# Gated cross-attention block on one core: attention by half pairs in batches of four units, one layer norm pass for the latents, and the first 2 MB over two DMA queues

## The chip, the cores and the metric

The kernel runs on one core of one Trainium2 chip. The metric is device time in microseconds (us): the median of the runs. The engines are TensorE (PE in the profile, its weight loads PEld), VectorE (DVE), ScalarE (ACT), GpSimd (POOL) and SyncE (SP), which here only issues DMAs.

## The reference, cut to what matters

Shapes: x is (2, 1024, 512), the context (2, 2048, 512), 16 heads of 64.

```python
x = x + tanh(g_xattn) * xattn(_layernorm(x), ctx)          # (x - m) / sqrt(var + 1e-5)
x = x + tanh(g_ffn) * ffn_int8(_layernorm(x))              # quantised 512x512 product

# inside xattn
lat = layer_norm(latents, g, b)                            # a second norm of the normed x, then gain and bias
ctx = layer_norm(context, g, b)
q = lat @ Wq                                               # 512 -> 1024
k, v = split(ctx @ Wkv)                                    # 512 -> 2048; k gets rotary cos/sin
attn = clip(q k^T / 8, -11, 11)
out = softmax(attn) v
return out @ Wo + bo
```

So x is normalised twice in a row before q. With v the variance of x and e = 1e-5, the two passes together multiply (x - m) by 1/sqrt(v(1 + e) + e^2).

## The kernel before

Everything is float32. Products that need the precision are split: a tensor is held as a rounded part (`_hi`, type float32r) and a rest (`_lo`), and three float32r products are summed (`split_product`). The probabilities, values and row sums are plain float32, and the profile shows each such matmul as two.

There are four stages, each with a hand-written program for every engine, joined by semaphores.

**Query stage.** x comes in four chunks of 512 rows into `raw`. For each chunk DVE measures mean and variance (`measure`, bn_stats and bn_aggr), ACT takes the root (`sqrt`), DVE normalises in place (`normalise`), and all that a second time, since the reference does it twice. PE transposes the chunk into `turn_ps` (`turn`), ACT applies gain and bias (`affine`), DVE splits the result into `tok_hi` and `tok_lo` (`tok_split`), and PE makes eight q tiles of 128 columns from it. The first chunk is handled in two parts (one tile of 128 rows, then three). Wq arrives in two stages of 1 MB, each with half of the 512 rows and all 1024 columns; ACT makes `wq_hi` and POOL `wq_lo`, and the first q product waits for both stages. All loads are issued by SP. ACT first computes `gate_tanh`.

**Context stage.** Eight chunks of context give k and v, which go to scratch in DRAM. The change touches it only in names and in one place of ACT's program.

**Attention stage.** Two batches by eight pairs of heads give 16 head pairs (`ALLPAIRS`). A head pair has 16 steps of 128 keys, each against all 1024 queries. In step s, PE makes the scores of both heads (a = 0, 1) for the two query halves in two PSUM slots `score_ps[:, half]` (12 matmuls, two heads side by side on 64 rows of the array each), ACT takes the exponential of each half (128x1024) into `prob`, DVE clips the step's 128x2048 in place (`prob` L1022), PE multiplies with v (`value_ps` L874, two heads side by side on 64 columns each), and DVE adds the tile to `prob_sum` (L1013, L1016). `prob` has 4 slots, so DVE, ACT and PE may stand up to four steps apart. PE's order is scores(s), values(s-1).

After a head pair, PE sums `prob_sum` over the partitions (`sums`, L887), and the row sums take a way through DRAM: ACT copies them, SP stores them, loads them spread over 128 partitions, DVE takes reciprocals, SP stores these and loads them broadcast to 64 rows a head, DVE multiplies (`normalise`, L204), SP stores the output (`PairEnds`). SP issues the ten loads of pair n+2 (4 MB) when pair n is done, and then this chain.

In pairs 0 and 1 DVE also quantises the FFN weight (`quantise_rhs`), and POOL makes `wo_lo`.

**Output stage.** 16 tiles of 128 rows: projection by Wo, residual, norm, int8 product. The last pair's chain runs beside its first tiles.

## Time and profile before

| | us |
|---|---|
| median of 3 runs | 1541.34 |
| lowest, highest | 1540.91, 1545.64 |
| the profiled execution's own time | 1544.19 |
| its span | 1542.4 |
| PE busy | 1490.7 (97%) |
| DVE busy | 1287.8 (83%) |
| ACT busy | 714.5 (46%) |

PE's busy time counts matmuls that are pipelined, with ends that are modelled; it doesn't say that PE is at its peak. What a stretch costs is read from the starts of its instructions. The stages by time: query stage to about 130 us, context stage to 490, attention 492.5 to 1422, output stage to the end.

### The profile page before, as it was taken

What the parts mean: (1) busy time and instruction counts of PE and PEld (TensorE: products, weight loads), DVE (VectorE), ACT (ScalarE), POOL (GpSimd) and SP (SyncE); (2) the same over time, 40 slices, a digit from 0 to 9 for tenths busy, and PEclk for the clock granted to TensorE, in tenths of its full rate; (3) what the DMA queues carried; (4) which work ended last, traced back from release to release, by engine and by line L of the source; (5) the groups of instructions that cost most, each with busy time, mean ns of one, the idle gap of its engine ahead of it and who ended that gap; (6) DMA issues with size and microseconds to landing.
All of it is one profiled execution on the core that took longest, in us unless ns stands there. A gap on an engine that the chain in (4) does not pass through costs nothing. (4 is left out here: it accounts for less than half of the span.)

```text
span 1542.4 us, 22114 instructions
## 1 busy us (share of the span) xinstructions
PE 1490.7 (97%) x7896; PEld 869.5 (56%) x7896; DVE 1287.8 (83%) x1256; ACT 714.5 (46%) x794; POOL 127.8 (8%) x72
## 2 busy tenths in 40 slices
PE   3999999999999899999999999999999999999997
PEld 3788888888886334444444444444444444444774
DVE  6866666676654999899899899899899899998887
ACT  3433222222223555555555555555555555555342
POOL 2220000000000210000000000000000000000765
PEclk9999999999999999999999999999999999999998
DMA  5665655546567540541440440441441442311652
GB/s 185 232 240 190 190 164 181 161 153 200 163 181 256 142 123 29 124 115 38 123 123 28 123 123 27 123 123 38 113 123 46 105 123 55 97 42 35 185 163 82
DMA packets 121998, 195.30 MB, mean 127 GB/s; under 512 B 18368, under 2 KB 67520, under 8 KB 115808
## 3 DMA queue, kind: packets, MB, share of 16 engines
q1 hardware_dynamic: 119360, 190.49, 42.5%
q10 hardware_dynamic: 2592, 4.20, 0.7%
q8 instruction: 28, 0.46, 0.1%
q14 instruction: 18, 0.15, 0.0%
HBM read 114.70 MB, written 79.95 MB: 126 GB/s over the span
## 5 line engine op out<-in xcount | busy, mean ns | idle before, releaser
L932 ACT ACTIVATE prob<-score_ps 128x1024 f32<-128x1024 f32 x512 | 496.3, 1022 | 377.7 <-PE score_ps L861 377.5
L1016 DVE TENSOR_TENSOR prob_sum<-prob_sum,prob 128x2048 f32<-128x2048 f32 x224 | 516.0, 2304 | 0.5
L874 PE MATMUL value_ps<-prob,v_st 128*64 128x512 f32 x2048 | 496.6, 606 | 10.6 <-DVE prob L1022 10.3
L861 PE MATMUL score_ps<-q_st,k_st 64*128 64x512 f32 x3072 | 426.4, 409 | 2.5 <-PEq L102 2.1
L861 PEld LDWEIGHTS score_ps<-q_st,k_st 64*128 64x128 f32 x3072 | 269.2, 185 | 256.4 <-ACT prob L932 187.8
L1022 DVE TENSOR_SCALAR prob<-prob 128x2048 f32<-128x2048 f32 x256 | 314.0, 1226 | 68.1 <-ACT prob L932 64.2
L874 PEld LDWEIGHTS value_ps<-prob,v_st 128*64 128x64 f32 x2048 | 124.2, 136 | 250.1 <-issue 201.7
L645 DVE TENSOR_TENSOR k_cos<-k_raw,rope 128x1024 f32<-128x1024 f32 x32 | 39.2, 1225 | 99.9 <-ACT k_raw L546 99.9
L551 ACT ACTIVATE v_out<-proj_ps 128x1024 f32<-128x1024 f32 x31 | 31.9, 1030 | 136.7 <-PE proj_ps L228 136.7
L546 ACT ACTIVATE k_raw<-proj_ps 128x1024 f32<-128x1024 f32 x31 | 31.9, 1029 | 105.2 <-PE proj_ps L228 104.0
L1331 POOL MEMSET unround<- 128x1 f32 x1 | 0.1, 98 | 872.6 <-POOLq L115 872.6
L228 PE MATMUL proj_ps<-tok_hi,wkv_hi 128*128 128x512 f32 x248 | 67.0, 392 | 0.0
L228 PE MATMUL proj_ps<-wkv_lo,tok_hi 128*128 128x512 f32 x248 | 66.4, 389 | 0.0
L228 PE MATMUL proj_ps<-tok_hi,wkv_lo 128*128 128x512 f32 x248 | 66.3, 389 | 0.0
L228 PE MATMUL proj_ps<-tok_lo,wkv_hi 128*128 128x512 f32 x248 | 66.3, 389 | 0.0
L228 PE MATMUL proj_ps<-wkv_hi,tok_hi 128*128 128x512 f32 x248 | 66.3, 389 | 0.0
L228 PE MATMUL proj_ps<-wkv_hi,tok_lo 128*128 128x512 f32 x248 | 66.3, 389 | 0.0
L228 PEld LDWEIGHTS proj_ps<-tok_hi,wkv_lo 128*128 128x128 f32 x248 | 46.5, 188 | 9.7
L228 PEld LDWEIGHTS proj_ps<-wkv_hi,tok_lo 128*128 128x128 f32 x248 | 46.5, 188 | 9.7
L228 PEld LDWEIGHTS proj_ps<-wkv_lo,tok_hi 128*128 128x128 f32 x248 | 46.5, 188 | 9.7
L228 PEld LDWEIGHTS proj_ps<-wkv_hi,tok_hi 128*128 128x128 f32 x248 | 46.5, 188 | 9.7
L228 PEld LDWEIGHTS proj_ps<-tok_lo,wkv_hi 128*128 128x128 f32 x248 | 46.5, 188 | 9.7
(119 smaller groups left out, 1306.2 us busy)
## 6 DMA issues: line engine op xcount, KB each, us to landing
k_st<-k_scr SPq DMA_DIRECT2D x128, 256.0 KB, 6.2
k_scr<-k_hi SPq DMA_DIRECT2D x64, 256.0 KB, 2.7
v_scr<-v_out SPq DMA_DIRECT2D x32, 512.0 KB, 3.5
k_scr<-k_lo SPq DMA_DIRECT2D x64, 256.0 KB, 4.0
q_st<-q_scr SPq DMA_DIRECT2D x16, 1024.0 KB, 10.5
v_st<-v_scr SPq DMA_DIRECT2D x16, 1024.0 KB, 13.3
q_scr<-q_hi SPq DMA_DIRECT2D x32, 256.0 KB, 3.3
q_scr<-q_lo SPq DMA_DIRECT2D x32, 256.0 KB, 3.4
```

The costliest lines, as they stand in the source:

```text
L228: last = pe.matmul(acc, s, m, start=(n == 0), stop=(n == len(terms) - 1))
L546: act.activation(k_raw[:, j % 2, :, :], banks(what, j, order), ACT.Copy).then_inc(k_copied, 1)
L551: act.activation(v_out[:, j, :], banks(what, j, order), ACT.Copy).then_inc(v_copied, 1)
L645: last = dve.tensor_tensor(made[:, :, :], k_raw[:, s, :, :], rope[:, slot, f:f + 1, :].broadcast_to((P, 2, CH)), ALU.mult)
L861: last = pe.matmul(score_ps[:, half, a, :], k_st[slot][rows, k_part, s * P:(s + 1) * P], q_st[slot][rows, q_part, cols], start=(t == 0), s ...
L874: last = pe.matmul(value_ps[rows, cols], v_st[slot][:, s, rows], prob[:, s % PSLOT, a, cols], start=(s == 0), stop=(s == STEPS - 1))
L932: act.activation(prob[:, s % PSLOT, :, cols], score_ps[:, half, :, :], ACT.Exp, scale=SCALE).then_inc(exped, 1)
L1016: dve.tensor_tensor(total, total, prob[:, s % PSLOT, :, :], ALU.add).then_inc(added, 1)
L1022: dve.tensor_scalar(tile, tile, CLIP_LOW, CLIP_HIGH, ALU.max, ALU.min).then_inc(clipped, 1)
L1331: pool.memset(unround[:, :], -ROUND).then_inc(unround_set, 1)
```

## The change

Three things are changed at once.

**1. Attention.** The unit of work is now one step of 128 keys against 512 queries (one half), both heads. A head pair runs all 16 steps of query half 0, then all of half 1: 32 units, in 8 batches of 4. PE makes the scores of a batch (3 PSUM slots instead of 2, a wait on an exponential for each unit), then the values of the batch before. DVE clips a batch at once (128x4096) and adds it in two 128x2048 additions (one for the first batch of a half). `prob` has two slots of a batch. `value_ps` and `sum_ps` are half as wide. The additions keep two unit positions apart (j), so `sums` now runs four matmuls of 32 output columns for a half, at rows 0, 32, 64 and 96, and DVE joins the two parts before the reciprocal. The chain through DRAM runs twice a pair, once for a half, and SP issues the loads of pair n+2 between the two. `quantise_rhs` all falls into pair 0, three pieces a batch.

**2. Query stage.** One pass replaces the two norms: the root is taken of v(1 + e) + e^2. The first chunk goes tile by tile. wq_hi and wq_lo are now made by column halves (all 512 rows, 512 columns), so the first four q tiles wait only for the first half. DVE makes `wq_lo` instead of POOL. PE runs 56 transposes of the identity at the start (`keep_busy`), before the first tile is there, and 10 after the last transposed tile. The tanh of the gates moves to the end of the context stage.

**3. First loads.** The four tiles of the first chunk and the two halves of the first wq stage are issued in turns by SP and ACT.

```diff
-        for tiles, arrived in ((FRONT[0], front_in), (BACK[0], raw_in[0])):
-            sp.dma_start(raw[:, 0, tiles, :], ...
+        for t in range(0, CT, 2):
+            sp.dma_start(raw[:, 0, t, :], x[t * P:(t + 1) * P, :]).then_inc(front_in[t], 16)
+        load_stage(0)
         sp.dma_start(gains[:, :, :], affines).then_inc(gains_in, 16)
-        load_stage(0)
         load_stage(1)
...
     @block.scalar
+        for t in range(1, CT, 2):
+            act.dma_start(raw[:, 0, t, :], x[t * P:(t + 1) * P, :]).then_inc(front_in[t], 16)
+        load_wq_piece()
...
     @block.vector
-        for p in range(2):
-            measure(0, 0, p, p == 1, FRONT)
-            measure(0, 0, p, p == 1, BACK)
-            normalise(0, p, FRONT)
-            normalise(0, p, BACK)
+        for i, part in enumerate(SINGLE):
+            measure(0, 0, part)
+            if i:
+                normalise(0, 0, SINGLE[i - 1])
+        normalise(0, 0, SINGLE[-1])
+        wq_rest(0)
         tok_split(0, 0)
-        measure(1, 1, 2, False)
+        wq_rest(1)
+        measure(1, 1)
...
     @block.tensor
         pe.wait_ge(ident_set, 2)
-        turn(0, 0)
-        pe.wait_ge(w_hi_made, 2)
+        keep_busy(WARM_EARLY)
+        turn_singles()
+        keep_busy(WARM_LATE)
...
 attention, PE
-        def scores(n, slot, s):
+        def scores(n, slot, b):
-            for half in range(2):
-                g = 2 * (STEPS * n + s) + half
-                if not (first(n) and s == 0):
-                    pe.wait_ge(exped, g - 1)
+            for u in range(b * BATCH_UNITS, (b + 1) * BATCH_UNITS):
+                half, s = divmod(u, STEPS)
+                cols = slice(half * CH, (half + 1) * CH)
+                if u >= BANKS:
+                    pe.wait_ge(exped, UNITS * n + u - BANKS + 1)
...
-        def values(n, slot, s):
+        def values(n, slot, b):
+            pe.wait_ge(clipped, BATCHES * n + b + 1)
+            for i in range(BATCH_UNITS):
+                s = (b * BATCH_UNITS + i) % STEPS
                 for a in range(2):
+                    last = pe.matmul(value_ps[rows, :], v_st[slot][:, s, rows], prob[:, b % 2, i, a * CH:(a + 1) * CH],
...
+        def sums(n, half):
+            for j in range(2):
                 for a in range(2):
+                    row = (2 * j + a) * SUM_ROWS
+                    last = pe.matmul(sum_ps[row:row + SUM_ROWS, :], ones[:, 0:SUM_ROWS], prob_sum[:, half, j, a, :],
...
 attention, DVE
+        def clip(n, b):
+            tile = prob[:, b % 2, :, :]
+            dve.wait_ge(exped, UNITS * n + (b + 1) * BATCH_UNITS)
+            dve.tensor_scalar(tile, tile, CLIP_LOW, CLIP_HIGH, ALU.max, ALU.min).then_inc(clipped, 1)
...
 attention, SP
+        def after(n, where, before, loading=None):
+            ends.store_sums(sp, n, 0)
+            ends.load_sums(sp, n, 0)
+            if before is not None:
+                ends.store_output(sp, n - 1, 1, *before)
+            ends.store_reciprocals(sp, n, 0)
+            ends.load_reciprocals(sp, n, 0)
+            if loading is not None:
+                load(n + 2, *loading)
+            ends.store_sums(sp, n, 1)
+            ends.load_sums(sp, n, 1)
+            ends.store_output(sp, n, 0, *where)
+            ends.store_reciprocals(sp, n, 1)
+            ends.load_reciprocals(sp, n, 1)
```

PE's program at the start of the query stage, before. Each row is a line, an operation, output and inputs, the output's shape and how many in a row:

```order
L681 MATMUL turn_ps<-ident,raw 128x128 x4
L687 MATMUL turn_ps<-ident,raw 128x128 x12
L228 MATMUL proj_ps<-tok_hi,wq_hi 128x512 x4
L228 MATMUL proj_ps<-tok_hi,wq_lo 128x512 x4
L228 MATMUL proj_ps<-tok_lo,wq_hi 128x512 x4
```

And now:

```order
L684 MATMUL proj_ps<-ident 128x128 x56
L690 MATMUL turn_ps<-ident,raw 128x128 x16
L684 MATMUL proj_ps<-ident 128x128 x10
L230 MATMUL proj_ps<-tok_hi,wq_hi 128x512 x4
L230 MATMUL proj_ps<-tok_hi,wq_lo 128x512 x4
L230 MATMUL proj_ps<-tok_lo,wq_hi 128x512 x4
```

Transposes of the identity stand ahead of and behind the 16 of the first chunk; the q products are the same.

PE's program in pair 1 of the attention, around the sums of pair 0, before:

```order
L861 MATMUL score_ps<-q_st,k_st 128x512 x12
L874 MATMUL value_ps<-prob,v_st 64x512 x4
L887 MATMUL sum_ps<-prob_sum,ones 64x512 x4
L861 MATMUL score_ps<-q_st,k_st 128x512 x12
L874 MATMUL value_ps<-prob,v_st 64x512 x4
```

And now:

```order
L888 MATMUL score_ps<-q_st,k_st 128x512 x24
L900 MATMUL value_ps<-prob,v_st 64x512 x8
L888 MATMUL score_ps<-q_st,k_st 128x512 x24
L900 MATMUL value_ps<-prob,v_st 64x512 x8
L914 MATMUL sum_ps<-prob_sum,ones 32x512 x4
L888 MATMUL score_ps<-q_st,k_st 128x512 x24
L900 MATMUL value_ps<-prob,v_st 64x512 x8
```

Score and value matmuls now change places half as often, with 24 and 8 in a row for 12 and 4; the sums stand twice a pair, on 32 columns for 64.

DVE's program in a late pair of the attention, before:

```order
L1016 TENSOR_TENSOR prob_sum<-prob_sum,prob 128x2048
L1022 TENSOR_SCALAR prob<-prob 128x2048
L1016 TENSOR_TENSOR prob_sum<-prob_sum,prob 128x2048
L204 TENSOR_TENSOR o_out<-o_raw,recip 128x512
L1022 TENSOR_SCALAR prob<-prob 128x2048
```

And now, for the first half of a pair:

```order
L1050 TENSOR_SCALAR prob<-prob 128x4096
L1062 TENSOR_TENSOR prob_sum<-prob 128x2048
L1050 TENSOR_SCALAR prob<-prob 128x4096
L1066 TENSOR_TENSOR prob_sum<-prob_sum,prob 128x2048 x2
L206 TENSOR_TENSOR o_out<-o_raw,recip 128x512
L1050 TENSOR_SCALAR prob<-prob 128x4096
L1066 TENSOR_TENSOR prob_sum<-prob_sum,prob 128x2048 x2
L1050 TENSOR_SCALAR prob<-prob 128x4096
L1066 TENSOR_TENSOR prob_sum<-prob_sum,prob 128x2048 x2
L192 TENSOR_TENSOR sum_both<-sum_sq 128x8
L197 RECIPROCAL rec_sq<-sum_both 128x8
```

A half has 4 clips of double width and 7 additions; a whole pair had 16 clips and 15 additions.

## Rows read from the trace of the kernel before

**Rows 1.** Timeline of PE: start, us, engine, line, instructions; sums of pairs 1 and 5.

```profile
627.06 1.89 PE L887 MATMUL sum_ps<-prob_sum,ones 128*64 128x512 f32 x8
...
855.34 1.89 PE L887 MATMUL sum_ps<-prob_sum,ones 128*64 128x512 f32 x8
```

**Rows 2.** Timeline of one attention step; some rows from narrower windows.

```profile
803.54 1.65 PE L861 MATMUL score_ps<-q_st,k_st 64*128 64x512 f32 x12
804.35 0.62 PE L861 MATMUL score_ps<-q_st,k_st 64*128 64x512 f32 x4
804.58 0.19 PEld L861 LDWEIGHTS score_ps<-q_st,k_st 64*128 64x128 f32 x2
804.63 1.94 ACT L932 ACTIVATE prob<-score_ps 128x1024 f32<-128x1024 f32 x2 [0.67 <-PE score_ps L861]
805.13 1.94 PE L874 MATMUL value_ps<-prob,v_st 128*64 128x512 f32 x8
805.61 0.14 PEld L874 LDWEIGHTS value_ps<-prob,v_st 128*64 128x64 f32 x2 [0.29 <-issue]
806.04 0.14 PEld L874 LDWEIGHTS value_ps<-prob,v_st 128*64 128x64 f32 x2 [0.28 <-issue]
807.00 1.67 PE L861 MATMUL score_ps<-q_st,k_st 64*128 64x512 f32 x12
```

**Rows 3.** Timeline of DVE in the last pair, where an addition follows its own clip.

```profile
1377.24 1.22 DVE L1022 TENSOR_SCALAR prob<-prob 128x2048 f32<-128x2048 f32 x1
1378.49 2.29 DVE L1016 TENSOR_TENSOR prob_sum<-prob_sum,prob 128x2048 f32<-128x2048 f32 x1
...
1401.59 0.69 DVE L204 TENSOR_TENSOR o_out<-o_raw,recip 128x512 f32<-128x512 f32 x1
```

**Rows 4.** Timeline of pair 0 and the first sums.

```profile
492.52 1.66 PE L861 MATMUL score_ps<-q_st,k_st 64*128 64x512 f32 x12 [2.11 <-PEq L102]
506.21 4.47 DVE L1016 TENSOR_TENSOR prob_sum<-prob_sum,prob 128x2048 f32<-128x2048 f32 x1
567.55 1.89 PE L887 MATMUL sum_ps<-prob_sum,ones 128*64 128x512 f32 x8
```

**Rows 5.** DVE by line and form, 500 to 640 us: count, busy us, mean ns.

```profile
L985 DVE TENSOR_REDUCE rhs_amax<-rhs_raw 128x1 f32<-128x512 f32 x4 | 2.7, 670 | 0.0
L1001 DVE TENSOR_SCALAR rhs_raw<-rhs_raw 128x512 f32<-128x512 f32 x4 | 1.7, 415 | 0.0
```

**Rows 6.** Timeline of SP in one pair: sums stored, then loaded.

```profile
804.12 2.16 SPq L157 DMA_DIRECT2D sum_scr<-sum_row  x1
810.10 0.40 SPq L162 DMA_DIRECT2D sum_sq<-sum_scr  x1
```

**Rows 7.** Timeline of the query stage's start.

```profile
10.57 1.91 ACT L485 ACTIVATE wq_hi<-w_stage 128x2048 fp32r<-128x2048 f32 x1
10.91 1.46 DVE L592 TENSOR_SCALAR raw<-raw,meanvar,rstd 128x512 f32<-128x512 f32 x3
17.48 5.73 DVE L592 TENSOR_SCALAR raw<-raw,meanvar,rstd 128x512 f32<-128x512 f32 x3
27.93 2.04 PE L228 MATMUL proj_ps<-tok_hi,wq_hi 128*128 128x512 f32 x4 [1.84 <-DVE tok_hi L601]
34.54 1.09 PE L228 MATMUL proj_ps<-tok_hi,wq_lo 128*128 128x512 f32 x4
39.12 1.07 PE L228 MATMUL proj_ps<-tok_hi,wq_hi 128*128 128x512 f32 x4
```

**Rows 8.** Timeline of PE: the transposes of chunks 1 and 2.

```profile
44.56 1.91 PE L687 MATMUL turn_ps<-ident,raw 128*128 128x128 f32 x16
68.28 3.59 PE L687 MATMUL turn_ps<-ident,raw 128*128 128x128 f32 x16 [2.74 <-DVE raw L592]
```

**Rows 9.** Windows: PE, PEld, DVE, ACT, POOL busy us, PE clock, DMA share, GB/s.

```profile
68.00:71.00 3.00, 2.72 (x13) 2.72 (x14) 1.42 (x3) 1.49 (x2) 0.00 (x0) 0.54 1.01 380
71.00:74.00 3.00, 3.00 (x16) 2.60 (x15) 1.94 (x3) 1.61 (x3) 0.00 (x0) 0.89 1.04 386
```

More of the change, by code:

```diff
@@ L836, in _ @@
                 n = 2 * i + slot
-                load(n + 2, slot, sp.snap((n + 2) // PAIRS), sp.snap((n + 2) % PAIRS))
-                ends.fetch_reciprocals(sp, n)
-                ends.store_output(sp, n, sp.snap(n // PAIRS), sp.snap(n % PAIRS))
-        sp.wait_ge(late.o_stored, 16 * (ALLPAIRS - 2))
+                here, last, ahead = [(sp.snap((n + d) // PAIRS), sp.snap((n + d) % PAIRS)) for d in (0, -1, 2)]
+                after(n, here, last, (slot,) + ahead)
+        n = ALLPAIRS - 2
+        after(n, (BATCH - 1, PAIRS - 2), (BATCH - 1, PAIRS - 3))
+        for half in range(2):
+            sp.wait_ge(late.o_stored[half], 16 * PAIRS)
         for t in range(2):
@@ new lines, in spread_scales @@
+        def spread_scales():
+            pe.wait_ge(diag_made, KT)
+            pe.wait_ge(rhs_copied, 2)
+            for t in range(KT):
+                last = pe.matmul(row_ps[:, t * P:(t + 1) * P], ones[:, :], diag[:, t, :], start=True, stop=True)
+            last.then_inc(row_made, 1)
+        def pair(n, slot):
+            for b in range(BATCHES):
+                scores(n, slot, b)
+                if b >= 1:
+                    values(n, slot, b - 1)
+                elif not first(n):
+                    values(n - 1, 1 - slot, BATCHES - 1)
+                if b == 1 and not first(n):
+                    sums(n - 1, 1)
+                if b == HALF_BATCHES + 1:
+                    sums(n, 0)
+                if isinstance(n, int) and n == 1 and b in (2, 3):
+                    turn_rhs(b - 2)
+                if isinstance(n, int) and n == 1 and b == 4:
+                    spread_scales()
@@ new lines, in copy_values, with copy_sums @@
+        def copy_values(n, half):
+            act.wait_ge(valued, BATCHES * n + HALF_BATCHES * (half + 1))
+            if not first(n):
+                act.wait_ge(late.o_made, 2 * n + half - 1)
+            act.activation(late.o_raw[:, half * CH:(half + 1) * CH], value_ps[:, :], ACT.Copy).then_inc(late.o_copied, 1)
+        def copy_sums(n, half):
+            act.wait_ge(summed, 2 * n + half + 1)
+            if not (first(n) and half == 0):
+                act.wait_ge(late.sum_stored, 16 * (2 * n + half))
@@ new lines, in add_probs @@
+        def add_probs(n, b):
+            half, part = divmod(b, HALF_BATCHES)
+            total = prob_sum[:, half, :, :, :].rearrange("p j a c -> p j (a c)")
+            halves = [prob[:, b % 2, j:j + 2, :] for j in (0, 2)]
+            before = ADDS * (2 * n + half) + 2 * part - 1
+            dve.wait_ge(clipped, BATCHES * n + b + 1)
+            if part == 0:
+                if not first(n):
+                    dve.wait_ge(summed, 2 * (n - 1) + half + 1)
+                dve.tensor_tensor(total, halves[0], halves[1], ALU.add).then_inc(added, 1)
+                return
+            for j in range(2):
+                dve.wait_ge(added, before + j)
+                dve.tensor_tensor(total, total, halves[j], ALU.add).then_inc(added, 1)
@@ new lines, in pair @@
+        def pair(n, slot):
+            for b in range(BATCHES):
+                clip(n, b)
+                add_probs(n, b)
+                if b == 7 and not (isinstance(n, int) and n == ALLPAIRS - 1):
+                    ends.reciprocals(dve, n, 0)
+                if b == 1 and not first(n):
+                    ends.normalise(dve, n - 1, 0)
+                if b == 3 and not first(n):
+                    ends.reciprocals(dve, n - 1, 1)
+                if b == 5 and not first(n):
+                    ends.normalise(dve, n - 1, 1)
+                if first(n):
+                    for k in range(3):
+                        quantise_rhs(3 * b + k)
@@ L1293, in turn @@
             if isinstance(t, int) and t == 3:
-                ends.reciprocals(dve, LAST)
+                for half in range(2):
+                    ends.reciprocals(dve, LAST, half)
             ending = isinstance(t, int) and t == TILES + 1
```

430 lines of the change are left out of this document (197 added, 233 removed).

## The prediction

> **What bounds the kernel now.** I read three views in this order: the busy times, the timeline of PE at the sums of each pair, and the timeline of one attention step. The busy times put PE at 97% and DVE at 83%. The sums then give the beat of the longest stage: from 627.06 to 855.34 are four head pairs, 57.07 us each [rows 1], and every pair from the second to the fifteenth keeps that beat. A beat so regular, with no wait named ahead of PE's bursts, says that PE itself sets it.
>
> What is in it? A step takes 807.00 - 803.54 = 3.46 us [rows 2]: a score burst of 12 matmuls until 805.13, a value burst of 8 until the next scores. Inside a burst the matmuls go in twos. Two score matmuls take 0.23 us (804.35 to 804.58), two value matmuls 0.43 (805.61 to 806.04). Six twos and four twos are 1.38 + 1.72 = 3.10 us. So 0.36 us of each step is neither: it is lost where scores and values change places, 0.18 for each change. Sixteen steps are 55.3 us and the sums add the remaining 1.7, as much as a value burst without changes.
>
> DVE needs 1.25 us for a clip and up to 2.29 for an addition [rows 3], together 3.5 at most: it keeps step, with hardly anything to spare. At the two ends of the program PE isn't the bound: its first q product starts at 27.93 [rows 7], and pair 0 is late (below).
>
> **Attention, PE.** A pair has 32 units, each with three twos of scores and two twos of values: 0.69 + 0.86 = 1.55 us, 49.6 a pair, as before. There are 8 bursts of each kind for 16, so the changes cost 8 x 0.36 = 2.9 for 5.8. The sums are new in form: four matmuls of 32 output columns a half. Nothing in this trace runs four side by side. The value matmuls on 64 columns do run two side by side, at 0.43 for half a product each; so four matmuls cost 0.86 us if four run at once, and 1.72 if only two do. I take 0.86, since the twos are told apart by output rows alone and now there are four groups of rows, and 0.18 for one more change of form: 2.1 us a pair, at worst 3.8.
>
> One new wait stands in the middle of each score burst. The burst's fourth unit reuses the slot of its first, whose exponential starts 1.09 us after the burst and takes about 1.0 [rows 2]; it is free at about 2.1. Undisturbed, the fourth unit would start at 0.18 + 9 x 0.23 = 2.25, its weights a little before. That is just covered. I charge 0.2 us a pair, between nothing and 8 x 0.18 = 1.4. Sum: 49.6 + 2.9 + 2.1 + 0.2 = 54.8, which is 2.3 less than 57.1, and over 16 pairs 36.
>
> **Attention, DVE.** A short tensor_scalar (512 columns) takes 0.415 [rows 5], one of 2048 columns 1.22 [rows 3], so 4096 columns come to 1.22 + 0.81 x 2048/1536 = 2.30 us. Every operation now waits for the one before it, for which rows 3 show 0.03 (1.22 against 1.25 to the next start). A batch with two additions takes 2.33 + 2 x 2.32 = 6.97, one with a single addition 4.65; a pair 6 x 6.97 + 2 x 4.65 = 51.1, with two multiplications of 0.69 and the small reciprocals about 53.3. That is 1.5 below PE's 54.8. Within a half DVE falls behind: three batches of 6.97 against PE's 6.55, plus a multiplication and a reciprocal, against 1.04 for the sums; about 1.3 us of lag. The clip ends 7.4 us after its score burst began (1.1 + 4 x 1.0 + 2.3), its values are due at 6.55 + 2.94 = 9.5. So 2.1 us cover 1.3, and the light fourth batch restores the rest. PE stays the bound.
>
> **Attention, first pair.** Before, sums 0 came 75.0 us after the first scores [rows 4]. Eighteen steps and a score burst are 63.9, so 11 us were lost: DVE also quantises, and POOL's work beside it stretches single instructions (an addition took 4.47 for 2.29; there are four such places, 8.2 us together). Now all sixteen pieces fall into pair 0: 4 x 0.67 + 12 x 0.42 = 7.7. DVE's work is 51.1 + 7.7 + 8.2 = 67.0 from about 5 us after the first scores, so the clip of pair 1's first batch ends at 5 + 67 + 2.3 = 74.3. PE alone would want it after 10 score and 8 value bursts, 10 x 2.94 + 8 x 3.62 = 58.4. Lost: 16 us, against 11 then and 0.5 in pair 1. Charge 4.3, between -4 (no interference) and +8.
>
> **Query stage.** DVE's first pass over the first chunk ended at 10.91 + 1.46 = 12.37 and the second at 17.48 + 5.73 = 23.21 [rows 7]; from there the transposes, gain and bias and the split took 4.72 to the first product. Without the second pass the same tail starts at about 12.0 (tile by tile, a little sooner than 12.37) and ends at 16.6. ACT's half of wq was split by 12.48 already, and DVE's new piece of wq_lo (an addition's 2.29) lies beside ACT's gain and bias. Gain 27.9 - 16.6 = 11.3. The second weight half is wanted four tiles, some 11 us, later, and is covered.
>
> The first products ran slowly: 27.93 to 34.54 for four groups, against 39.12 - 34.54 = 4.58 for five. That lost 6.61 - 3.66 = 2.9. With the transposes ahead PE is warm, but it then stands idle for about 3 us before the first product, and after 2.74 idle the trace shows the clock at half (0.54, the 1.2 GHz level) and 16 transposes in 3.59 for 1.91 [rows 8, 9]. So 1.7 of the 2.9 are paid again: gain 1.2. That stall at 68.28 itself, a normalise that came late, has no cause left with half of the norm work: 2.74 + 1.68 = 4.4. Together 16.9.
>
> The Trainium skill (TensorE: Matmul & The Clock Gate, part 4, transpose) says that transposes don't count as activity for the clock gate. The trace speaks against it: from 68.28 PE ran only transposes, and the clock was back at full within 71 to 74 us (0.89 over that window, its first 0.6 us low) [rows 9]. By the page's rule the change would bring less, and it is a rival below.
>
> The loads over two queues give nothing of their own in this sum: the split of wq starts where ACT is free, at 10.57. The tanh lies in ACT's idle time (46% busy).
>
> **Sum.** 36 - 4.3 + 16.9 = 49. The durations are from the execution of 1544.19 us (span 1542.4), which is 2.85 above the median; that puts it at 1495, and the median at 1541.3 - 49 = 1492.
>
> **Rivals.** (a) The sums run only two side by side: 2 x 0.86 x 16 = 28 us more, 1520. For it: no row shows four. (b) The 0.18 of a change isn't the change but something that every unit pays, so that it doesn't shrink with the number of bursts: 2.9 x 16 = 46 more, 1538. Against it: two units stand in each burst of before, and 804.35 to 804.58 lies just behind the border between them, with no gap. (c) Transposes don't release the clock. Then 72 of them at 0.213 (3.59 / 16, rounded down for the warm end) last from about 2 to 17.4, the products start near 20.5 and run slowly at first: 3.9 + 1.7 more, 1498. The page of the skill named above is for it, rows 9 against. (d) Slower: DVE, which works strictly in order, waits at batch 3 for the sums of the second half. Their store now follows 4 MB of loads which themselves wait for the first half's reciprocals. Before, the store took 810.10 - 804.12 = 6.0 us behind the loads [rows 6]. Now I expect 12, so the sums arrive about 30 us into the next pair, and DVE asks at 33. From 34 on each us late costs 16; the gain is gone from 37, 7 us later than I expect. If the way through DRAM takes 11 more, the time is 1492 + 16 x 4 = 1556. (e) DVE's interference with POOL vanishes and the fourth unit waits for nothing: 1481.
>
> **How the numbers follow.** Forecast 0.60 with a range of its own of 1482 to 1503, (a) 0.12, (b) 0.06, (c) 0.10, (d) 0.06, (e) 0.06. Change of less than 0.3% (1537 to 1546) can't be told from none: that is (b), 0.06. Slower is (d), 0.06. Faster 0.88. The range takes in (e), the forecast and (c) whole and the better part of (a), where three of the four groups might overlap: 1479 to 1518; (b), (d) and the rest of (a) lie outside.
>
> **What would show it.** The sums of half 1 must stand 54.8 us apart; 56.5 means (a), and the sum matmuls' starts then lie 0.43 apart in twos. Value bursts of 8 matmuls' worth must run 3.5 us without a gap, score bursts 2.8. A wait of PE for an exponential in mid burst prices the fourth unit. DVE waiting for a DMA ahead of the joining addition is (d). The first product should start at 16 to 17, and its first groups show the clock. I am wrong if the pair stays above 56 us.

## The result, and the profile after

The changed kernel takes 1487.96 us (median of 5 runs, 1487.20 to 1490.23) against 1541.34 before: a ratio of 0.965, 95% interval 0.9635 to 0.9665. The prediction said 1492, 1479 to 1518. The profiled execution took 1489.53 us (span 1487.7, before 1542.4). The spans differ by 54.7, and the two traces divide that so:

| stretch | before | after | difference | forecast |
|---|---|---|---|---|
| start to first scores | 492.5 | 474.9 | -17.6 | -16.9 |
| head pair in the loop, times 16 | 57.07 | 54.57 | -40.0 | -36 |
| rest of the attention (pair 0 above all) | 16.5 | 20.7 | +4.2 | +4.3 |
| behind the last sums | 120.3 | 119.0 | -1.3 | 0 |

The third row holds more than pair 0: the code of the last two pairs stands outside the loop, and from pair 14's first sums (1292.59) to pair 15's (1347.81) are 55.2 us instead of 54.57.

Timeline of PE in a loop pair, the answer to [rows 1] and [rows 2] (start, us, engine, line, instructions):

```profile
801.04 1.06 PE L914 MATMUL sum_ps<-prob_sum,ones 128*32 128x512 f32 x8
802.04 3.05 PE L888 MATMUL score_ps<-q_st,k_st 64*128 64x512 f32 x24
805.02 3.65 PE L900 MATMUL value_ps<-prob,v_st 128*64 128x512 f32 x16
808.60 3.07 PE L888 MATMUL score_ps<-q_st,k_st 64*128 64x512 f32 x24
...
828.36 1.07 PE L914 MATMUL sum_ps<-prob_sum,ones 128*32 128x512 f32 x8
...
855.63 1.07 PE L914 MATMUL sum_ps<-prob_sum,ones 128*32 128x512 f32 x8
```

The weight loads (PEld) of a burst's fourth unit, once in the loop and once in pair 14:

```profile
804.12 0.53 PEld L888 LDWEIGHTS score_ps<-q_st,k_st 64*128 64x128 f32 x6 [0.17 <-ACT prob L966]
...
1295.77 0.53 PEld L888 LDWEIGHTS score_ps<-q_st,k_st 64*128 64x128 f32 x6 [0.25 <-ACT prob L966]
```

Two halves take 855.63 - 801.04 = 54.59 us. Measured by starts, a score burst of 24 takes 2.98 and one of 12 took 1.59 [rows 2]; twelve more cost 1.39, so 0.20 of each burst doesn't depend on its length. For values it is 3.58 and 1.87: eight more cost 1.71, and 0.16 is left. Together 0.36 for each pair of changes of form, as forecast. The sums take 802.04 - 801.04 = 1.00 for a half, so four matmuls of 32 columns do run side by side. No PE row in the loop waits for an exponential, but the weights of the fourth unit wait 0.17 us for one in every burst. It hardly lengthens the burst: 2.98 to 3.02 from start to start.

DVE over the same pair (one row of the windows view: stretch, length, then busy us of PE, PEld, DVE, ACT, POOL, clock, DMA share, GB/s), and the way of the sums of a second half, which [rows 6] show for before:

```profile
801.04:855.60 54.56, 54.56 (x338) 25.81 (x336) 51.74 (x29) 32.59 (x36) 0.00 (x0) 1.00 0.39 97
```

```profile
830.34 8.88 SPq L160 DMA_DIRECT2D sum_scr<-sum_row  x1
...
843.02 0.39 SPq L165 DMA_DIRECT2D sum_sq<-sum_scr  x1
...
848.06 0.16 DVE L192 TENSOR_TENSOR sum_both<-sum_sq 128x8 f32<-128x8 f32 x1
```

The store, behind 4 MB of loads, holds the next step up for 12.7 us; the load lands 1.9 us after its issue, at 844.9, which is 29.7 us into the pair (first scores at 815.18). DVE asks at 32.9. The forecast had 30 and 33.

Timeline of PE at the start, against [rows 7], and windows of it:

```profile
2.12 8.81 PE L684 MATMUL proj_ps<-ident 128*128 128x128 f32 x56 [2.12 <-POOL ident_bf L465]
10.77 1.91 PE L690 MATMUL turn_ps<-ident,raw 128*128 128x128 f32 x16
12.52 1.25 PE L684 MATMUL proj_ps<-ident 128*128 128x128 f32 x10
16.12 1.17 PE L230 MATMUL proj_ps<-tok_hi,wq_hi 128*128 128x512 f32 x4 [2.34 <-DVE tok_hi L599]
17.12 1.58 PE L230 MATMUL proj_ps<-tok_hi,wq_lo 128*128 128x512 f32 x4
...
21.47 1.07 PE L230 MATMUL proj_ps<-tok_hi,wq_lo 128*128 128x512 f32 x4
...
23.29 1.07 PE L230 MATMUL proj_ps<-tok_hi,wq_hi 128*128 128x512 f32 x4
```

```profile
2.10:7.20 5.10, 5.08 (x24) 5.08 (x25) 2.92 (x12) 2.08 (x4) 0.00 (x0) 1.00 0.94 338
...
17.50:20.90 3.40, 3.40 (x10) 2.44 (x9) 3.40 (x3) 0.43 (x1) 0.00 (x0) 0.50 0.34 134
```

Up to 7.2 us 24 transposes take 0.21 us each, from start to start. From then on they take 0.11 (the other 32 until 10.77). PE has done nothing but transposes by that time. The clock column says 1.00 in both stretches, so at the very start of an execution the count must be read and not the column. The clock is back at half from 17.5 to 20.9, after PE's idle time up to 16.12.

The first pair: DVE beside POOL, what ScalarE and PE wait for, and the clip of pair 1's first batch (546.94):

```profile
480.80 2.29 DVE L1050 TENSOR_SCALAR prob<-prob 128x4096 f32<-128x4096 f32 x1 [11.97 <-ACT prob L966]
...
488.03 6.68 DVE L1066 TENSOR_TENSOR prob_sum<-prob_sum,prob 128x2048 f32<-128x2048 f32 x2
489.03 3.53 POOL L1093 TENSOR_TENSOR wo_lo<-wo_raw,wo_hi 128x1024 fp32r<-128x1024 f32 x1 [4.50 <-ACT wo_hi L1004]
...
504.85 1.06 ACT L1004 ACTIVATE wo_hi<-wo_raw 128x1024 fp32r<-128x1024 f32 x1 [5.59 <-DMA wo_raw<-wo_dram]
505.82 3.75 ACT L966 ACTIVATE prob<-score_ps 128x1024 f32<-128x1024 f32 x4
506.88 0.97 PE L888 MATMUL score_ps<-q_st,k_st 64*128 64x512 f32 x6 [2.78 <-ACT prob L966]
...
546.94 2.29 DVE L1050 TENSOR_SCALAR prob<-prob 128x4096 f32<-128x4096 f32 x1
...
549.28 3.66 PE L900 MATMUL value_ps<-prob,v_st 128*64 128x512 f32 x16 [1.40 <-DVE prob L1050]
```

Two additions that take 4.62 elsewhere take 6.68 beside POOL: 2.06 us lost, and that four times. DVE is busy for 40.8 of the 41.1 us from 480.80 to 521.90. The values of pair 1's first batch, at 549.28, wait for that batch's clip and stand 74.4 us after the first scores (474.89); the forecast said 74.3. Part of this agreement is luck: DVE's first clip came at 5.9 instead of 5, and its work took 68.4 instead of 69.3 (67.0 and the clip). Of the 5.9, 1.1 belong to the clock, which stood at half (0.50) from 475.0 to 478.3. In the run without warming it didn't fall there, the first clip came at 4.8, and the same values stand at 73.3. But ScalarE stands in the same stretch too: it works in order, and the load of wo holds back its next exponentials. The forecast didn't name that.

### The profile page after: what moved, and what is told of

Same layout as the page of the kernel before. It is cut to its first block and busy times, and to the rows that moved or that the text cites. A ratio compares the mean times of both kernels' runs of the same rounds, so it can differ in the third digit from the quotient of the medians.

```text
span 1487.7 us, 22575 instructions
## 1 busy us (share of the span) xinstructions
PE 1458.5 (98%) x8090; PEld 886.2 (60%) x8090; DVE 1246.0 (84%) x1108; ACT 706.5 (47%) x823; POOL 118.7 (8%) x71
## 5 line engine op out<-in xcount | busy, mean ns | idle before, releaser
L966 ACT ACTIVATE prob<-score_ps 128x1024 f32<-128x1024 f32 x512 | 483.1, 1032 | 187.1 <-PE score_ps L888 184.3
L900 PE MATMUL value_ps<-prob,v_st 128*64 128x512 f32 x2048 | 468.6, 599 | 4.9 <-DVE prob L1050 4.9
L1066 DVE TENSOR_TENSOR prob_sum<-prob_sum,prob 128x2048 f32<-128x2048 f32 x192 | 446.3, 2325 | 13.6 <-DVE prob L1050 0.2
L888 PE MATMUL score_ps<-q_st,k_st 64*128 64x512 f32 x3072 | 396.7, 403 | 7.9 <-ACT prob L966 5.8
L888 PEld LDWEIGHTS score_ps<-q_st,k_st 64*128 64x128 f32 x3072 | 272.8, 186 | 177.5 <-issue 103.1
L1050 DVE TENSOR_SCALAR prob<-prob 128x4096 f32<-128x4096 f32 x128 | 292.7, 2287 | 41.0 <-ACT prob L966 38.8
L900 PEld LDWEIGHTS value_ps<-prob,v_st 128*64 128x64 f32 x2048 | 135.8, 137 | 272.9 <-issue 265.0
L1062 DVE TENSOR_TENSOR prob_sum<-prob 128x2048 f32<-128x2048 f32 x32 | 75.8, 2368 | 1.8 <-DVE prob L1050 0.2
L979 ACT ACTIVATE sum_row<-sum_ps 128x512 f32<-128x512 f32 x32 | 19.2, 599 | 93.4 <-PE sum_ps L914 93.4
```

Source lines behind the costliest of these rows:

```text
L888: last = pe.matmul(score_ps[:, u % BANKS, a, :], k_st[slot][rows, k_part, s * P:(s + 1) * P], q_st[slot][rows, q_part, cols], start=(t == ...
L900: last = pe.matmul(value_ps[rows, :], v_st[slot][:, s, rows], prob[:, b % 2, i, a * CH:(a + 1) * CH], start=(s == 0), stop=(s == STEPS - 1))
L966: act.activation(prob[:, b % 2, u % BATCH_UNITS, :], score_ps[:, u % BANKS, :, :], ACT.Exp, scale=SCALE).then_inc(exped, 1)
L979: act.activation(late.sum_row[:, :], sum_ps[:, :], ACT.Copy).then_inc(late.sum_copied, 1)
L1050: dve.tensor_scalar(tile, tile, CLIP_LOW, CLIP_HIGH, ALU.max, ALU.min).then_inc(clipped, 1)
L1062: dve.tensor_tensor(total, halves[0], halves[1], ALU.add).then_inc(added, 1)
```

## Experiments

Each ratio is against the kernel before, with its 95% interval. In the diffs, what stands behind a # is added for the reader. Differences between two of these kernels are given from their medians and, where the effect is small, from their traces.

**The attention part alone.** The changed kernel with `projections` as before.

> The query and context stages are those of the kernel before; only the attention part (batches of four units, sums four side by side) is the changed one. My theory: the attention and the start are two separate gains that add up. 16 pairs x 2.50 us shorter, less 4.2 us lost in pair 0, less about 1 at the end: 1541 - 37 = 1504, and the 17 us that are then missing against the changed kernel (1488) are the whole worth of the query stage. Rival: part of the gain is shared (pair 0 meets another state of the buffers and of the clock when it starts 17 us sooner), then the time is away from 1504 by several us, 1500 or 1508.

Measured: 1505.79 us, ratio 0.9767 (0.9751 to 0.9783). That leaves 1505.8 - 1488.0 = 17.8 us for the query stage; the attention alone came within 2 us of the 1504 expected. In the two traces the query stage is worth less: the first scores stand at 490.29 here and at 474.89 in the changed kernel, 15.4 apart, and not 17.6 as against the profiled execution of the kernel before. Its trace shows how much of [rows 8] was chance:

```profile
67.74 1.97 PE L689 MATMUL turn_ps<-ident,raw 128*128 128x128 f32 x16 [2.75 <-DVE raw L594]
69.47 1.17 PE L230 MATMUL proj_ps<-tok_hi,wq_hi 128*128 128x512 f32 x4
```

With the same query stage, PE waits the same 2.75 us for the normalised chunk, but here the clock doesn't fall, and the 16 transposes take 1.97 instead of 3.59. So the stall costs 4.4 us in one execution and 2.8 in another, and 1.6 of the table's 17.6 are chance.

**One queue for the first loads.**

```diff
-        for t in range(0, CT, 2):
+        for t in range(CT):
             sp.dma_start(raw[:, 0, t, :], ...
...
-                for k in range(1 if w == 0 else 2):
+                for k in range(2):
...
-        for t in range(1, CT, 2):
-            act.dma_start(raw[:, 0, t, :], ...
-        load_wq_piece()
```

> The changed kernel with all of x's first chunk and wq's first half on SP's queue, none on ScalarE's. My theory: DVE works through the four tiles one by one (0.69 + 0.18 + normalising each), and the queues share the same 16 DMA engines, so the two queues bring little: +0 to +1 us against the changed kernel, 1488 to 1489, the first product at 16.1 to 17. Rival: it is the issue on one queue that spaces the tiles; then tile 3 and wq arrive 2 us or more later, the first product stands at 18 or more, and the time is 1490 or more.

Measured: 1487.97 us, ratio 0.9652 (0.9635 to 0.9668): no difference. The first tile is measured at 4.65 instead of 4.11, DVE waits 0.73 us once for a tile, and the first product starts at 16.63 instead of 16.12. Two queues are worth half a microsecond at the first product, which the run times can't show.

**No warming transposes; more of them.** `WARM_EARLY = 0, WARM_LATE = 0`, and `WARM_LATE = 28`.

> The changed kernel without the 56 + 10 transposes of the identity ahead of and behind the first chunk's own. My theory: they release the clock. Without them the 16 turned tiles run at the 1.2 GHz level (0.21 us each for 0.12; only the last tile's four lie on the path: +0.4), and the first products lose the 2.9 us that the kernel before lost instead of about 1.7: +1.6 in all, 1489.6; the clock record first reaches 1.0 some 6 us after the first product. Rival, by which transposes don't count: the time stays at 1488.0. A second rival: the products' slow start costs more than before because 3 more groups fall in it: 1491.

> The changed kernel with 28 instead of 10 transposes between the last turned tile and the first product, so that PE (idle from 13.77 to 16.12 in the changed kernel) has work until about 15.9 us. My theory: the fall to the 1.2 GHz level from 17.50 to 20.91 was the answer to that idle time; it goes away, the first groups run at full speed and the time is 1.7 us less: 1486.3. Rival: the fall has another cause (a change from transposes to products), then the fall stays, the time is 1488.0, or a little more if the 28 end after the tokens are there.

Measured: 1487.70 (0.9649, 0.9633 to 0.9665) and 1487.84 (0.9651, 0.9635 to 0.9667). As times neither differs from 1487.96; the traces can be read up to the first scores. Without warming:

```profile
15.70 2.05 PE L230 MATMUL proj_ps<-tok_hi,wq_hi 128*128 128x512 f32 x4 [4.51 <-DVE tok_hi L599]
17.55 1.91 PE L230 MATMUL proj_ps<-tok_hi,wq_lo 128*128 128x512 f32 x4
19.25 1.72 PE L230 MATMUL proj_ps<-tok_lo,wq_hi 128*128 128x512 f32 x4
20.81 1.08 PE L230 MATMUL proj_ps<-tok_hi,wq_hi 128*128 128x512 f32 x4
```

With 28 behind the tiles:

```profile
12.79 3.22 PE L684 MATMUL proj_ps<-ident 128*128 128x128 f32 x28
16.38 1.16 PE L230 MATMUL proj_ps<-tok_hi,wq_hi 128*128 128x512 f32 x4 [0.38 <-DVE tok_hi L599]
17.39 1.08 PE L230 MATMUL proj_ps<-tok_hi,wq_lo 128*128 128x512 f32 x4
...
20.56 1.07 PE L230 MATMUL proj_ps<-tok_hi,wq_lo 128*128 128x512 f32 x4
```

Against 0.91 us for a group of four at full speed, the slow start costs 2.4 without warming (15.70 to 20.81 for three groups), 1.7 in the changed kernel (16.12 to 21.47 for four) and 0.5 with 28 (16.38 to 20.56; the clock stays up, what is lost is two short waits). The same start with 10 transposes, in the run "DVE busier" below:

```profile
16.43 1.17 PE L232 MATMUL proj_ps<-tok_hi,wq_hi 128*128 128x512 f32 x4 [2.35 <-DVE tok_hi L601]
...
20.62 1.08 PE L232 MATMUL proj_ps<-tok_hi,wq_lo 128*128 128x512 f32 x4
```

Here PE is idle for 2.35 us and the clock stays up all the same (1.00 from 16.4 to 24.0); four groups take 4.19, as with 28. Eight traces of this case have the 10 transposes and 2.3 to 2.7 us of idle time: in seven the clock falls, in this one it doesn't. In the three traces with 28 or 36 transposes, where PE is idle for 0.4 to 0.8 us, it doesn't fall there. So transposes do release the clock (0.21 to 0.11 above, and products at full speed right behind the 28), and the idle time before the first product mostly, but not always, gives it back. The size that I expected for the first, 1.6 us, wasn't seen as a whole: 0.7 were paid, and the first product even came 0.4 sooner, because the 56 transposes of the changed kernel end at 10.8 and hold back the turned tiles (the last tile is normalised at 10.0). Without warming PE was also idle for 4.51 us ahead of the products, so the 0.7 doesn't separate the two effects. The first scores stand at 475.16, 474.89 and 473.98 in the three traces.

**A pair of matmuls more, in the value burst or in the score burst.** A helper adds two value-form matmuls, in four of eight bursts a pair, once beside the values, once between the second and third unit of the scores.

```diff
+        def filler(slot):
+            for a in range(2):
+                rows = slice(a * DHEAD, (a + 1) * DHEAD)
+                pe.matmul(value_ps[rows, :], v_st[slot][:, 0, rows], ..., start=False, stop=False)
...
+                if u % BATCH_UNITS == 2 and b % HALF_BATCHES >= 2:
+                    filler(slot)                      # in scores; in the control:
+                if i == 2 and b % HALF_BATCHES in (1, 2):
+                    filler(slot)                      # in values
```

> The changed kernel with one more pair of value-form matmuls (64 output columns, moving 512 columns of v, start and stop both off, so that it adds wrong values to the output) in the middle of four of a head pair's eight value bursts: 4 x 16 = 64 pairs more, no change of form more. Theory: each costs the 0.43 us of two value matmuls, of which pair 0, where PE waits anyway, hides its four: 60 x 0.43 = 25.8 to 64 x 0.43 = 27.5, so 1514 to 1515.5. It is the control of the next kernel.

> The same 64 pairs of value-form matmuls (output wrong in the same way), now each in the middle of a score burst, between its second and third unit, so that scores change to values and back twice more often there: 128 changes more. Theory (a change of form costs 0.18 us whatever its place): 60 to 64 times 0.36 above the kernel with the pair in the value burst, 22 to 23 us, 1536 to 1538. Rival (what the larger bursts save is something else, a start-up that each batch pays, such as waiting for ScalarE or the semaphores of a burst): the two kernels take the same, 1515. Between the two the difference prices a change: difference / 122.

Measured: 1539.62 us (0.999, 0.9981 to 1.000) and 1558.17 (1.0111, 1.0094 to 1.0128). The control was mis-sized by two: each float32 matmul is two on the array (x4 in the row for two calls), so a pair costs 0.86, not 0.43, and 60 x 0.86 = 51.6 is the measured 51.7. Their difference, 18.6, is what the pair of kernels was made for; 22 to 23 were expected. Where it comes from is seen in one batch of the second:

```profile
802.01 1.66 PE L896 MATMUL score_ps<-q_st,k_st 64*128 64x512 f32 x12
803.60 1.08 PE L878 MATMUL value_ps<-v_st 128*64 128x512 f32 x4
804.61 1.67 PE L896 MATMUL score_ps<-q_st,k_st 64*128 64x512 f32 x12
806.22 3.65 PE L908 MATMUL value_ps<-prob,v_st 128*64 128x512 f32 x16
```

From 802.01 to 806.22 are 4.21 us. The undivided burst takes 2.98 and the pair 0.86, 3.84 together. Two changes of form cost 0.37. Over a whole head pair the difference is smaller than 4 x 0.37 = 1.5: the loop's period is 59.33 for 58.00, that is 0.33 for two changes, since undivided score bursts take 2.97 to 2.98 in this kernel and 2.98 to 3.02 in the control and the changed kernel. Pair 0 hides its share. The rival, a start-up that each batch pays whatever its form, would give no difference and is out, and with it the prediction's rival (b).

**The sums two side by side.**

```diff
-                    row = (2 * j + a) * SUM_ROWS
-                    last = pe.matmul(sum_ps[row:row + SUM_ROWS, :], ones[:, 0:SUM_ROWS], prob_sum[:, half, j, a, :],
-                                     start=True, stop=True)
+                    rows = slice(a * DHEAD, (a + 1) * DHEAD)
+                    last = pe.matmul(sum_ps[rows, :], ones[:, 0:DHEAD], prob_sum[:, half, j, a, :],
+                                     start=(j == 0), stop=(j == 1))
```

> The changed kernel with the sums on 64 output columns, two side by side, as before the change; the two parts are added in PSUM. Theory: four side by side take 0.86 + 0.18 us, two side by side twice the 0.86: 32 x 0.86 = 27.5 us more, less what pair 0 hides (0.9), so 1514.5 to 1515.5, and a head pair takes 54.57 + 1.72 = 56.3. Rival: with PE slower DVE's lag shrinks and PE gets some back, or the sums lie under a wait: then a head pair is below 56.0 and the time under 1511.

The diff leaves out one line: DVE joins the two loaded rows by their maximum instead of their sum, since both now hold the same sum.

Measured: 1510.36 us, ratio 0.9803 (0.9786 to 0.9819): 22.4 more than the changed kernel, where I expected 27.5, and a head pair of 55.99.

```profile
801.60 3.65 PE L900 MATMUL value_ps<-prob,v_st 128*64 128x512 f32 x16
805.09 1.89 PE L914 MATMUL sum_ps<-prob_sum,ones 128*64 128x512 f32 x8
806.90 3.05 PE L888 MATMUL score_ps<-q_st,k_st 64*128 64x512 f32 x24
```

The sums take 1.81 for 1.00, and the value burst ahead of them 3.49 for 3.58: on 64 columns the sums have the form of the values, so a change is saved. That is 2 x (0.81 - 0.09) = 1.44 a pair, 23 in all. I had left out the change that goes away.

**wo_lo made by DVE.** The four subtractions move from POOL's program to DVE's, behind the additions of the same batches.

> The changed kernel with the four subtractions that make wo_lo on DVE (behind the additions of the same batches), none on POOL. Theory (POOL's instruction holds DVE up for about 2.1 us each, DVE needs 1.2 for the same work, and pair 0 is bound by DVE): 4 x (2.1 - 1.2) = 3.6 us less, 1484.4, and no DVE instruction of pair 0 is longer than its like elsewhere, but for the one beside bo_gated. Rival: pair 0 is bound by its loads and by the order of ScalarE's work, so moving the work to DVE adds 4 x 1.2: 1493.

Measured: 1485.22 us, ratio 0.9638 (0.9622 to 0.9654), 2.7 less than the changed kernel by the medians; the intervals overlap, so the time alone isn't proof. The trace bears the theory out in kind: the additions take 4.62 throughout and wo_lo 1.22. The sums of pair 1's first half stand 104.4 us after the first scores, for 107.8, but 1.1 of these 3.4 are the clock, which didn't fall at the first scores here. Counted from DVE's first clip to the second half's sums, pair 0 takes 69.9 for 72.1: 2.2 us less, where 3.6 were expected. The rival (slower) is out. What is missing is a new wait of DVE for the exponentials, and PE's grew too:

```profile
506.38 1.65 PE L888 MATMUL score_ps<-q_st,k_st 64*128 64x512 f32 x6 [4.07 <-ACT prob L966]
...
518.28 2.29 DVE L1050 TENSOR_SCALAR prob<-prob 128x4096 f32<-128x4096 f32 x1 [1.47 <-ACT prob L966]
```

That is ScalarE's wait for wo, no longer hidden by DVE's lag.

**The sums of the second half later.** Two extra loads, one behind the other, ahead of the one that counts.

```diff
+        for k in range(DETOURS if half == 1 else 0):
+            sp.dma_start(late.sum_sq[:, half, :, :], ...).then_inc(late.detour, 16)
+            sp.wait_ge(late.detour, 16 * (DETOURS * n + k + 1))
```

> The changed kernel in which the sums of each pair's second half, once stored in DRAM, are loaded three times one behind the other (two detours, then the load that DVE waits for). In the trace of the changed kernel the one load is issued at 843.02, takes 1.9 us, and DVE takes the sums at 848.06, 32.9 us after the pair's first scores at 815.18. Theory (the rival of the slower kernel in the prediction, (d), whose way was right and whose 3 us of cover were there): two detours of some 2.9 us make the sums 2.7 us late, of which the first 1 costs nothing: 14 to 16 times 1.7, 24 to 27 us more, 1512 to 1515, with DVE waiting for a DMA ahead of the joining addition. Rival (DVE's idle 1.3 us a pair and the clip's cover take it all up): under 3 us more, 1488 to 1491.

Measured: 1489.38 us, ratio 0.9654 (0.9639 to 0.9669): 1.4 more, no difference that the intervals show. The expectation failed on a price, the 2.9 us of a detour:

```profile
845.66 0.37 SPq L171 DMA_DIRECT2D sum_sq<-sum_scr  x1
...
847.61 0.17 DVE L198 TENSOR_TENSOR sum_both<-sum_sq 128x8 f32<-128x8 f32 x1 [0.68 <-DMA sum_sq<-sum_scr]
```

The sums arrive 33.6 us into the pair (first scores 814.01) instead of 29.7, so a detour cost 1.95. DVE waits 0.68 us, and the pair still takes 54.6. It shows the cover of 3 us ahead of DVE's question, and that a wait under 1 us costs nothing, as the prediction's rival (d) had it (nothing lost up to 34, one past DVE's question at 33). What each microsecond beyond costs wasn't reached and stays untested.

**DVE busier.** Each normalising product is done two times more, into a spare tile, 2.66 us a pair.

> The changed kernel with each normalising product on DVE (128 x 512, 0.69 us, 0.61 to the next start) done two times more into a spare tile, four more a pair from pair 1 on: 2.5 to 2.6 us more of DVE's time a pair. Theory: DVE stands idle for 1.3 to 1.5 us of a pair's 54.57 in the changed kernel, and PE is the bound by just that; what is over turns DVE into the bound: (2.6 - 1.4) x 14 = 17 us more (14 to 20), 1502 to 1508, a head pair of 55.7 to 55.9. Rival 1: DVE has no slack, since its order and the clip's due time use it up: 2.6 x 15 = 39 more, 1527. Rival 2: DVE is far from the bound: 1488.

Measured: 1500.05 us, ratio 0.9723 (0.9708 to 0.9738): 12.1 more, where 17 were expected. DVE waits for nothing any more in the pair from 830 to 886, and PE waits for it:

```profile
826.89 3.65 PE L902 MATMUL value_ps<-prob,v_st 128*64 128x512 f32 x16 [0.67 <-DVE prob L1052]
...
854.62 3.65 PE L902 MATMUL value_ps<-prob,v_st 128*64 128x512 f32 x16 [0.40 <-DVE prob L1052]
```

From pair 1's to pair 15's first sums a pair takes 55.4 on the average (1356.89 - 581.2 over 14), in the changed kernel 54.65. So 2.66 more of work cost 0.76, and the slack was 1.9 us a pair, more than the 1.3 to 1.5 that I read from DVE's waits. In the loop alone a pair takes 55.47 (802.45 to 1301.72 are nine) for 54.57, which makes it 1.8. Both rivals are out: PE is the bound by just 1.8 to 1.9 of 54.6.

**A faster kernel, first try.** wo_lo on DVE; of the rhs quantisation the scaling and the shift on ScalarE; `WARM_EARLY = 34`, `WARM_LATE = 36`.

> A try at a faster kernel: the changed one with (1) wo_lo made on DVE, as in the run before, measured 2.7 us; (2) of the rhs quantisation's 12 short operations on DVE in pair 0 the 8 that scale and shift are given to ScalarE (four behind batch 6 of pair 0, four behind batch 0 of pair 1): 8 x 0.38 = 3.0 us off DVE, where it bounds pair 0; (3) 34 instead of 56 warming transposes ahead of the first tile, since in the changed kernel the turned tiles wait behind them (10.77 to 12.68, though the last tile was normalised at 10.0, and ScalarE free at 11.6): 0.85 us sooner; 36 instead of 10 behind it, so that the clock doesn't fall: 1.2 us. Theory: all of it adds up: 1488.0 - 2.7 - 3.0 - 0.85 - 1.2 = 1480.2 (1479 to 1482). Rival: in pair 0 something else than DVE's work is by then the bound (ScalarE behind batch 6, 4.0 + 4 x 0.5 us): then (2) gives nothing and the time is 1483 to 1484.

Measured: 1487.54 us, ratio 0.964 (0.9626 to 0.9654): no gain that the intervals show. The start did as expected (first product 15.10, clock up, first scores at 472.70 for 474.89), and the span is shorter by that much, 1485.6 for 1487.7. In pair 0 the rival won, and harder than I had put it:

```profile
504.48 1.65 PE L890 MATMUL score_ps<-q_st,k_st 64*128 64x512 f32 x6 [3.50 <-ACT prob L968]
...
511.62 1.06 ACT L1018 ACTIVATE wo_hi<-wo_raw 128x1024 fp32r<-128x1024 f32 x1 [4.43 <-DMA wo_raw<-wo_dram]
...
540.29 2.56 ACT L991 ACTIVATE rhs_int<-rhs_raw,shift 128x512 bf16<-128x512 f32 x4 [2.54 <-DVE rhs_raw L1052]
...
544.30 1.42 PE L890 MATMUL score_ps<-q_st,k_st 64*128 64x512 f32 x6 [2.40 <-ACT prob L968]
```

**Second try.** The same work, placed where its input is there. The diff is against the first try.

```diff
-    WO_BATCHES = (1, 3, 4, 5)
+    WO_TURNS = ((0, 2), (0, 4), (0, 6), (1, 0))       # (pair, batch), ACT and DVE
...
-                if isinstance(n, int) and (n, b) in ((0, 6), (1, 0)):
+                if isinstance(n, int) and (n, b) in ((0, 7), (1, 1)):
                     shift_rhs(n == 1)
...
-            if k in (3, 5, 7, 9):
+            if k in (6, 9, 12, 15):                   # one reduction a batch
```

> The kernel of the run before with what was in its way in pair 0 taken apart. Its trace showed ScalarE, which works in order, waiting for the loads of wo (4.43 us at 511.62) and for DVE's clipped rhs (2.54 at 540.29), each time with the exponentials of the next batch behind it, and PE waiting 3.50 and 2.40 for those. Now the four pieces of wo are split two batches apart (behind batches 2, 4 and 6 of pair 0 and 0 of pair 1, on ScalarE and DVE), the four reductions of rhs stand one each in batches 2 to 5, ScalarE scales behind batch 7, DVE clips in pair 1's batch 0, ScalarE shifts behind pair 1's batch 1; the diagonals move to pair 1's batch 0. Theory: pair 0 is then bound by DVE's own work alone, 51.1 + 2.6 for the reductions + 3 x 1.2 for wo_lo = 57.3 for 67 in the changed kernel, of which pair 1 gets 2.6 back: 6.5 us less in the pairs 0 and 1, 2.2 less at the start (15.10 for 16.12, no fall of the clock), 1488.0 - 8.7 = 1479.3, and the sums of pair 0's second half stand 71.5 us after the first scores, for 78.0. Rival: the wait only moves (SP is in order too: the sums of pair 0's first half are stored behind the third piece's load): then PE waits for DVE behind batch 7 and the time is 1483 or more.

Measured: 1481.59 us, ratio 0.9608 (0.9595 to 0.9621). Its interval lies wholly below the changed kernel's (0.9635 to 0.9665): 6.4 us less, by the medians 59.8 less than before. 1479.3 was expected, 8.7 less; the rival (1483 or more) is out. The values of pair 1's first batch:

```profile
537.91 3.65 PE L902 MATMUL value_ps<-prob,v_st 128*64 128x512 f32 x16 [0.40 <-DVE prob L1059]
541.50 1.07 PE L916 MATMUL sum_ps<-prob_sum,ones 128*32 128x512 f32 x8
```

The sums stand 541.50 - 472.93 = 68.6 us after the first scores, for 78.0; expected was 71.5. Pair 1 gives 2 us of the 9.4 back (PE waits 1.85 at 546.71 for ScalarE, whose shift of rhs waits for DVE). By the spans of the traces the kernel gains 9.2, by the medians 6.4. The changed kernel's profiled execution lay 1.6 above its median, which is more than half of the difference between the two; another 1.4 lie outside the span (time less span is 3.2 here and 1.8 there).

## Why the prediction was right

The mechanism was right, and so was the size of nearly every term. By the spans the change brought 54.7 us for a forecast 49: 3.7 of the difference from the head pairs, 0.7 from the query stage, 1.3 from behind the last sums.

- **The changes of form.** 0.36 us for each pair of changes, halved in number: measured 0.36 by the bursts' lengths, and 0.33 to 0.37 by the experiment that puts two changes in. Shown. The Trainium skill (TensorEngine Tiling (Array Packing), Key Properties) says that changing the tiling mode drains TensorE; it gives no price. The trace fits that with about 0.18 us lost at a change; what the array does meanwhile no row shows.
- **The sums four side by side.** Forecast 1.04 a half, measured 1.00; the experiment that undoes them costs 22.4 us. Rival (a) is out, and its price of 28 was too high by the change of form that two side by side don't need.
- **The fourth unit's wait.** Charged 0.2 a pair, measured next to nothing in the loop: twelve twos of 0.23 [rows 2] and 0.20 for the form are 2.96 of the burst's 2.98. With the sums' 0.1 that is the mis-sized term of the sum: 54.8 for 54.57, 0.23 x 16 = 3.7 us of the 5.7. The wait was "just covered", as the prediction put it: 0.17 us on the weights, nothing on PE's rows.
- **DVE beside PE.** Forecast DVE 1.5 below PE; measured slack 1.8 to 1.9. Right in kind, and the sums' way through DRAM came within 0.3 us of its forecast. One sum of rival (d) is wrong by its own rule: sums that come 11 us later than expected are 7 past the 34 from which each costs 16, so 1492 + 112 = 1604, not 1556. It touches neither the range nor a chance, and no run shows what a late microsecond costs.
- **The first pair.** Forecast 4.3 more, measured 4.2 for all that isn't a loop pair or an end, and the values of pair 1's first batch at 74.4 for 74.3. That DVE's work bounds the pair was right: from its first clip to the second half's sums it takes 72.0 to 72.1 us in the changed kernel and in the traces of four others whose pair 0 is the same, whatever the clock did. That the numbers agree to 0.1 is partly luck, as said above. What was missing is ScalarE's wait for wo, hidden in this kernel behind DVE's lag. It took back 1.5 us when wo_lo moved to DVE, and everything that the first faster kernel should have gained in pair 0.
- **The query stage.** First product at 16.12 for 16.6; from there to the seventh group 7.17 for 8.47, 1.3 of a forecast 1.2; from the 25th to the 61st group 36.09 for 40.66, the stall of 4.4 gone (4.6). Sum 17.6 for 16.9. Of the 4.4, 1.6 belong to a fall of the clock that another execution of the same stage doesn't have, so with that execution the stage gains 15.4 and the forecast is 1.5 too high. The fall after the idle time before the first product was taken as certain; it came in seven traces of eight.
- **Rival (c)**, by which transposes don't release the clock. The Trainium skill (TensorE: Matmul & The Clock Gate, part 4, transpose) says so. Here the trace speaks against it again: after 24 transposes at 0.21 us they take 0.11, with no product yet run, and products right behind 28 transposes start at full speed. By the page's rule warming with transposes would change nothing; without it the first three groups of products are slow (2.4 us lost, against 1.7 and 0.5). The price of it all is under 2 us, though, so a mistake here would hardly have moved the forecast.
- **Queues.** Nothing was charged, and the run times show nothing; the trace shows half a microsecond at the first product.
- Behind the last sums 1.3 us were gained that no term had; I didn't trace them.

## What to carry to other kernels

Fit burst lengths of two sizes (12 and 24, 8 and 16) before you price a batching change: the part that doesn't scale is what batching saves. When work is moved off the engine that lags, look at every in-order engine beside it for a wait that the lag has hidden, and place the moved work behind the landing of its load, not where there is a free slot. And keep the margin of the second engine in sight: with PE 2.5 us a pair faster, DVE has 1.8 to 1.9 us left, and by the run "DVE busier" a further gain on PE beyond that should bring nothing. Before you read a difference of 1 or 2 us out of two traces, look whether the clock fell in one of them.

## What the runs showed of the hardware

- A float32 addition on DVE is held up 2.05 to 2.09 us by a 128x1024 subtraction on POOL (a pair of additions 6.68, 6.68 and 6.71 for 4.62, a single one 4.34 for 2.29). On DVE the same subtraction takes 1.22. The Trainium skill (SBUF — State Buffer, SBUF: two separate sides) calls the port pair that the two share an exclusive lock. The trace fits that: the loss is nearly the same four times, beside POOL rows of 3.05 to 4.13 us, and it is more than the whole work costs DVE.
- The clock can fall in the middle of the attention. In the changed kernel it stands at half (1.2 GHz) from 515.8 to 519.3, after PE waited 2.78 and 2.23 us for ScalarE (0.51 in the window). The value burst in it takes 4.44 us for 3.58. DVE is busy all through it, so here the time didn't grow by that. In the last experiment, where no wait of PE in pair 0 is longer than 1.1, it doesn't fall there. But it doesn't in the run with the sums two side by side either (1.00 from 500 to 530), where PE waited 3.10 and 1.78: waits of this length make a fall likely, not certain.
- The same score burst takes 2.98 us in the loop and 3.07 to 3.09 in the pairs whose code stands outside it (first and last two). The rows show where the 0.07 to 0.09 sit: the weights of the fourth unit wait 0.25 us for the exponential there, 0.17 in the loop, and the burst's first exponential starts 1.10 us after it (1294.69 against 1293.59) for 1.00 (803.04 against 802.04). Why ScalarE starts later there is open.
